# One feed forward moved from an X phase to a Y phase, and the first norm of layer 0 applied after the transpose

## The reference

```python
emb = silu(_sin_emb(timestep)) @ W_ada + b_ada
scale, shift = split(emb)                       # one pair of rows per sequence
x = _ln(src) * (1.0 + scale) + shift            # the first norm; x is also the residual
q, k, v = heads(x @ Wq + bq), heads(x @ Wk + bk), heads(x @ Wv + bv)
scores = q / sqrt(16) @ k.T + attention_bias    # (4, 16, 512, 512), read from HBM
probs = softmax(where(src_mask, -inf, scores))
x = x + (probs @ v) @ Wo + bo
h = _ln(x) * g2 + beta2
x = x + (z * sigmoid(1.702 * z)) @ W2 + b2      # z = h @ W1 + b1, 1024 wide
```

## Time and profile before

| what | before |
|---|---|
| median of 3 runs | 956.56 us |
| lowest, highest | 955.17, 959.86 us |
| the profiled execution, its own time | 951.38 us |
| its span | 949.7 us |
| mean granted clock of PE | 0.935 of full |

### The profile page before, as it was taken

The page is one execution under the profiler, slowest core; times in us unless marked ns, Lnnn a source line. Parts: engine busy times, 40 slices in busy tenths (PEclk is TensorE's granted clock), DMA queues, the critical chain, the costliest instruction groups (busy, mean ns, idle before and its releaser), DMA issues.

```text
span 949.7 us, 14619 instructions
## 1 busy us (share of the span) xinstructions
PE 816.6 (86%) x4856; PEld 488.1 (51%) x4856; DVE 584.7 (62%) x1677; ACT 493.9 (52%) x881; POOL 424.8 (45%) x437
## 2 busy tenths in 40 slices
...
GB/s 237 175 224 250 268 264 178 150 123 146 163 137 2 1 68 156 116 197 224 173 146 45 2 114 173 126 209 202 130 48 46 45 68 150 29 1 2 1 23 22
DMA packets 80046, 114.75 MB, mean 121 GB/s; under 512 B 7691, under 2 KB 43359, under 8 KB 79971
## 3 DMA queue, kind: packets, MB, share of 16 engines
...
## 4 chain that ended last, share of the span: by engine, by line
PE 60%; DVE 17%; issue 7%; ACT 6%; DMA 4%; POOL 3%; SPq 2%; DVEq 0%; ACTq 0%
PE psD L924 11%; PE psD L936 11%; PE psE L958 7%; PE psC L971 5%; PE psS L950 4%; PE psC L1016 4%; PE psD L896 4%; DMA qk<-work 3%; PE psD L912 3%; DVE tiles L1374 3%; POOL tiles L561 2%; PE psS L986 2%; PE psE L1004 2%; PE psD L903 2%; DVE junk L1389 2%
## 5 line engine op out<-in xcount | busy, mean ns | idle before, releaser
L561 POOL TENSOR_TENSOR tiles<-tiles,mask_neg 128x512 f32<-128x512 f32 x256 | 300.3, 1203 | 62.3 <-DMA tiles<-in_fside_Bx16xSxS 47.2
L1374 DVE CUSTOM_DVE_ANT_0 tiles<-psS,tiles 128x512 f32<-128x512 f32 x256 | 173.7, 687 | 131.8 <-PE psS L950 115.0
L696 ACT ACTIVATE prob<-psE 128x512 f32<-128x512 f32 x256 | 151.5, 598 | 88.8 <-PE psE L958 81.6
L687 ACT ACTIVATE tiles<-tiles,rmax 128x512 f32<-128x512 f32 x224 | 162.3, 726 | 48.2 <-DVE rmax L1374 47.5
L958 PE MATMUL psE<-ident,tiles 128*128 128x128 f32 x1024 | 159.1, 278 | 10.9 <-ACT prob L696 10.5
L958 PEld LDWEIGHTS psE<-ident,tiles 128*128 128x128 f32 x1024 | 125.7, 143 | 61.8 <-ACT prob L696 29.5
L936 PE MATMUL psD<-w,work 128*128 128x256 f32 x512 | 132.9, 386 | 3.4 <-ACT hT L739 2.4
L924 PE MATMUL psD<-hT,w 128*128 128x512 f32 x256 | 127.3, 618 | 9.3 <-DVE work L1340 5.9
L602 POOL TENSOR_SCALAR_AFFINE_SELECT prob<-prob 128x256 f32<-128x256 f32 x128 | 50.1, 415 | 185.4 <-ACT prob L708 185.4
L1389 DVE CUSTOM_DVE_ANT_0 junk<-psS,later 128x128 bf16<-128x128 f32 x192 | 82.2, 443 | 76.2 <-PE psS L986 75.5
L950 PE MATMUL psS<-qk 96*128 96x512 bf16 x256 | 100.5, 395 | 22.7 <-DVE rmax L1374 15.4
...
## 6 DMA issues: line engine op xcount, KB each, us to landing
tiles<-in_fside_Bx16xSxS SPq DMA_DIRECT2D x256, 256.0 KB, 3.0
...
qk<-mT SPq DMA_DIRECT2D x64, 3.0 KB
...
```

The costliest lines, as they stand in the source:

```text
L561: pool.tensor_tensor(tile(b, s), tile(b, s), mask_neg[:, tile_of(s)[1], :], ALU.add).then_inc(masked, 1)
L687: act.activation(tile(b, s), tile(b, s), ACT.Identity, scale=-1.0, bias=rmax[0][:, s:s + 1]).then_inc(shifted_a, 1)
L696: act.activation(prob0[:, part_no % 2, j, :, s % 2 * P:(s % 2 + 1) * P], psE[:, e_no(0, b, s) % 2, :].rearrange("p (k q) -> p k q", k=T), ...
L1374: dve.tensor_tensor_reduce(tile(b, s), psS[:, n % 2, :], tile(b, s), 1.0, -3e38, ALU.add, ALU.max, rmax[0][:, s:s + 1]).then_inc(s_drained, 1)
```

## The change

1. **Plan.** The FFN of layer 0, sequence 1, stands in Y0 (slots 20 to 54) and no longer in X1. In Y0 the transposes T1 go from slot 31 to 57, QK from 33, 37, 41, 45 to 58, 61, 64, 67, V from 46, 48 to 72, 76, T2 from 29 to 19. In X1 T1 goes from 49 to 30, QK from 50, 52, 54, 56 to 32, 36, 40, 44, V from 58, 60 to 50, 54. Other phases have slots moved a little. ("ahead of that phase's projections": F1 and F2 are issued before T1 and QK.)
2. **First norm of layer 0.** DVE writes only the normed rows, into `xh` (`normalise`, as in all other norms). PE transposes `xh`; ACT applies scale and shift while it drains, from `ada_col`, a turned copy of scale and shift that four small transposes at the start make for all sequences. The residual `res[b]` is now made on POOL (`modulate`): `xh` times scale, bias of O added to the shift row, and that row added. DVE's next norm waits until POOL and PE have read `xh`.
3. **Start.** `ada_rows(0)` and `keep_ada(0)` stand behind the QK products, the mask of sequence 0 (`turn_mask`) behind `normalise`, and the POOL memsets behind `inv_std`.
4. **SP.** In Y0 and Y1 the first half of the role copies stands ahead of the last `max_rows`. The weights of the next FFN are loaded in Y0.

```diff
 ("start", 0)
-  pre=(0, 0), ln=0, ada=0, t1=2, qk=4, qk_by=2, v=(12, 14)
+  pre=(0, 0), ln=0, ada=11, t1=2, qk=4, qk_by=2, v=(12, 14)
 ("Y", 0)
-  tail=(0, 1), turn=2, out=(9, 10), ln2=13, t2=29, x1=53, masks=41, pre=(0, 2), ln=19, ada=14, t1=31, qk=33, qk_by=4, v=(46, 48)
+  tail=(0, 1), turn=2, out=(9, 10), ln2=13, t2=19, ffn=(0, 1), f1=(20, 22, 24, 26, 28, 30, 32, 34), step=0, f2=(37, 46), per=2, x1=56, masks=44, pre=(0, 2), ln=22, ada=17, t1=57, qk=58, qk_by=3, v=(72, 76)
 ("X", 1)
-  tail=(1, 0), turn=4, out=(9, 13), ln2=17, t2=27, ffn=(0, 1), f1=(1, 3, 5, 7, 10, 13, 15, 17), step=0, f2=(17, 29), per=2, pre=(1, 1), ln=40, t1=49, qk=50, qk_by=2, v=(58, 60)
+  tail=(1, 0), turn=2, out=(9, 13), ln2=17, t2=27, pre=(1, 1), ln=22, t1=30, qk=32, qk_by=4, v=(50, 54)
...
 in_y (SP):
-                if at.ffn and b < B - 1:
+                if at.ffn and at.ffn[0] and b < B - 1:
                     store(at.ffn[1])
+                if at.pre and not at.pre[0]:
+                    to_roles(*at.pre, 0)
                 max_rows(b, 3)
...
                 if at.pre:
-                    for c in range(C):
-                        to_roles(*at.pre, c)
+                    if at.pre[0]:
+                        to_roles(*at.pre, 0)
+                    to_roles(*at.pre, 1)
 POOL:
+            def modulate(b):
+                pool.wait_ge(norm_ready, T * (NORMS.index((0, b, 0)) + 1))
+                wait_emptied(pool, 0, b, "ada", 0)
+                pool.tensor_tensor(res[b][:, :, :], xh[:, :, :], ada[:, 0:D].unsqueeze(1).to_broadcast([P, T, D]), ALU.mult).then_inc(rows_scaled, 1)
+                pool.wait_ge(rows_in, N_ROWS)
+                pool.tensor_tensor(ada[:, D:2 * D], ada[:, D:2 * D], bo_all[0][:, :], ALU.add).then_inc(shift_set, 1)
+                pool.wait_ge(rows_scaled, b + 1)
+                pool.wait_ge(shift_set, b + 1)
+                add_row(res[b], res[b], ada[:, D:2 * D], bo_added)
...
                 inv_std(l, b, 0)
                 if not l:
-                    yield at.t1 + 2
-                    add_bo(b)
+                    yield at.t1 + 2 if at.tail else STEPS - MASK_AHEAD
+                    modulate(b)
 ACT, keep_turned:
-                        scale, shift = 1.0, 0.0
+                        scale, shift = (ada_col[:, x * C + c, b:b + 1] for x in range(2))
 DVE, normalise:
+                if n and half == 0:
+                    pl, pb, second = NORMS[n - 1]
+                    wait_bank(dve, pl, pb, "T2" if second else "T1", C - 1)
+                    if not pl and not second:
+                        dve.wait_ge(rows_scaled, pb + 1)
 DVE, projections:
-                        yield max(at.ln + 4, at.ada + 2) + 2 * half
-                        modulate(b, half)
+                        yield max(at.ln + 4, at.t2 + 2 if at.tail else 0) + 2 * half
+                        normalise(0, b, 0, res[b], half)
```

More of the change, by code:

```diff
@@ L83 @@
 PLANS = {
-    ("start", 0): Plan(pre=(0, 0), ln=0, ada=0, t1=2, qk=4, qk_by=2, v=(12, 14)),
-    ("X", -1): Plan(pre=(0, 1), ln=3, ada=5, t1=14, qk=16, qk_by=4),
-    ("X", 0): Plan(tail=(0, 0), turn=5, out=(9, 10), late=(0, 1, (3, 4)), ln2=13, t2=18, ffn=(0, 0), f1=(21, 22, 24, 25, 27, 28, 31, 31), step=0, f2=(34, 41), per=3.0, pre=(1, 0), ln=50, t1=57, qk=58, qk_by=2, v=(65, 67)),
-    ("Y", 0): Plan(tail=(0, 1), turn=2, out=(9, 10), ln2=13, t2=29, x1=53, masks=41, pre=(0, 2), ln=19, ada=14, t1=31, qk=33, qk_by=4, v=(46, 48)),
@@ new lines @@
+    ("X", -1): Plan(pre=(0, 1), ln=6, ada=5, t1=14, qk=16, qk_by=4),
+    ("X", 0): Plan(tail=(0, 0), turn=5, out=(9, 10), late=(0, 1, (3, 4)), ln2=13, t2=18, ffn=(0, 0), f1=(21, 22, 24, 25, 27, 28, 31, 31), step=0, f2=(34, 43), per=3.0, pre=(1, 0), ln=50, t1=57, qk=58, qk_by=2, v=(65, 67)),
+    ("Y", 0): Plan(tail=(0, 1), turn=2, out=(9, 10), ln2=13, t2=19, ffn=(0, 1), f1=(20, 22, 24, 26, 28, 30, 32, 34), step=0, f2=(37, 46), per=2, x1=56, masks=44, pre=(0, 2), ln=22, ada=17, t1=57, qk=58, qk_by=3, v=(72, 76)),
```

73 lines of the change are left out of this document (33 added, 40 removed).

## The result

| | before | after |
|---|---|---|
| median, same chip, 4 runs each | 955.87 us (952.57 to 959.86) | 944.38 us (940.15 to 946.79) |
| ratio, with its 95% interval | | 0.9877 [0.9852, 0.9902] |
| profiled execution: time, span | 951.38, 949.7 us | 943.82, 942.1 us |
| mean granted clock of it | 0.935 | 0.944 |

The forecast was 938.7 us, 926 to 953: faster, as forecast, and inside the range, but by 11.5 us of the medians (7.6 of the two profiled spans) where 17.9 were forecast. The ratios rest on undisturbed executions alone, and since the one profiled execution of experiment 1's kernel was a slow one (954.23 us), no phase of it is used.

A forecast was written before the change was run, and what follows sets the result against it. TensorE was taken as full in X1, with room in Y0, where DVE was crowded and the clock low. Terms -23.6 + 10.0 - 2.3 - 0.7 - 1.3 = -17.9 gave 933.5 us profiled, 938.7 as median; range 926 to 953.

The forecast's parts named there:

- the two large terms: X1 without the feed forward, -23.6 us, and Y0 with it, +10.0 us.
- the small ones: Start -2.3 us, X-1 -0.7 us, and Y1 with the boundary to X2 -1.3 us.
- 82.6 / 0.886: X1: PE's remaining work of 82.6 us over the busy share 0.886 from X-1 between 72 and 131 us, giving 93.2 us.
- X1 over 100: X1: a sign that the forecast is wrong, if the phase lasts over 100 us; 90 to 97 would show it right.
- I take these to cancel: Y0: twelve split instructions of DVE leave the crowded stretch, the gates' 10.4 us replace them; net effect put at nothing.
- the 3 us on top of Y1: Y0: added to Y1's 97.2 us for gates on DVE, the second norm's earlier transposes and POOL's modulation, giving 100.2 us.
- The slower rival: Y0: the feed forward runs at the low clock, 55.4 us for 27.7; Y0 +40, total 968.7 us; chance 0.05.
- a clock of 0.5 in Y0's FFN: Y0: a sign that the forecast is wrong, TensorE's granted clock at 0.5 during the feed forward.
- Start, -2.3 forecast: Start: eight modulation instructions become four and the mask moves behind, 1.5 + 1.5 us saved; the ada copy costs 0.7.
- X-1, -0.7 forecast: X-1: a POOL bias add of 2.4 us leaves the mask stream; modulation and mask at the end cost 1.7.
- that rival: Y0: PE waits 7 us for max rows behind six role copies on SyncE, total 945.7 us; chance 0.04.
- GpSimd's passes hold DVE: Rival: POOL's longer norm passes stop DVE 3 us at each of four places, 12 us, total 950.7; chance 0.04.

The follow-up runs named there:

- experiment 1: The kernel after with the feed forward back in X1 (Y0 and X1 plan rows of before, T2 of Y0 at 19), new norm kept: 947.29 us, 0.9914 of before.
- experiment 2: The kernel before with only the feed forward moved to Y0 (X1's norm at slot 24), norm and start as before: 956.62 us, 1.0028 of before.
- experiment 3: The kernel after with X1's norm at slot 24 in place of 22: 944.41 us, 0.9896 of before.
- experiment 8: The kernel after with X1's norm at slot 24 and 20 useless matmuls keeping TensorE busy at the X0 to Y0 boundary: 944.90 us, 0.9867 of before.

## Why the prediction was right, and where its terms were off

- **Direction and range: right.** It came out of two errors that partly cancel. Against the forecast sum of -17.9, the two large terms gave +1.7 in place of -13.6, the small ones -9.2 in place of -4.3. That the time fell inside the range is in part luck: with the large terms as measured and the small ones as forecast, the sum is -2.6 and the time 954.0 us, just outside it. The forecast's main mechanism, that the move gives most of the gain, was wrong: by experiment 2 the move alone gives none.
- **X1, -23.6 forecast, -15.0 measured: mis-sized.** The step was "82.6 / 0.886". PE's work, 82.6, is 84.7 where the clock held (experiment 3) and 88.1 where it fell. The share is 0.862 and 0.866, between X-1's whole (0.83) and its good part (0.886) in the earlier trace rows. I had taken the clock of that good part, 1.00, with the share. In X1, with the feed forward gone, PE waits up to 1.93 us at a time for DVE's maxima where two norms meet, and in that stretch the clock falls: 3.6 us of the 8.6 missing, by experiment 3's X1; that the waits make it fall is not shown. The bound of -15.2, X-1's whole length, is what came. The condition "X1 over 100" of the wrong side was met, at 101.8; it holds in executions with the dip, not in those without.
- **Y0, +10.0 forecast, +16.7 measured: mis-sized.** Two steps failed. "I take these to cancel" was said of the projections that move to slots 58 to 76. I had argued there from DVE's idle time alone; the part after slot 56 got 8.7 us longer for 7.6 us more PE work. The forecast took Y1's length, and Y1's part behind about its slot 56 is 28.6 us, Y0's now 33.6. And the 3 us on top of Y1 did not contain the clock at Y0's beginning: it is 0.50 after 4.6 us of standing still at the boundary, 1.6 to 2.9 us by experiment 8, and at half clock again for the first F1 group, 1.9 us. Y0 came out 9.7 us over before's Y1 (97.2), and 5.0, up to 2.9 and 1.9 us are about that; that they add up so is an estimate, not shown.
- **The slower rival** (the feed forward at the low clock) is right in its mechanism for one group out of eight; from 290 us on the clock was 0.96 and over, as I had said would show the forecast right. It had put 40 us on Y0. By this one group the sign "a clock of 0.5 in Y0's FFN" was met as well.
- **Start, -2.3 forecast, -2.4 measured: right in size, one of two steps did not pay.** Four norms in 1.38 us in place of eight instructions in 3.5 us gave 2.1. The mask's 1.5 us off the path gave nothing, since the norm starts at 18.55 us where the modulation started at 18.52. In its place stand one short DVE instruction on the mask's rows (L1233), which lasted 1.32 us instead of 0.18, until GpSimd's memset beside it ended (at 16.63 us; by the change the memsets stand behind `inv_std`), and the copy of the turned ada columns, 0.22 us of wait and 0.18. The transposes end 1.8 us earlier, the last split of q and k 1.4 us, and the other 1.0 us came behind it, between that split and the first scores, where the role copies run; why is open.
- **X-1, -0.7 forecast, -5.6 with X0: wrong in its cause.** I priced GpSimd's passes and left DVE's own length at nothing. From X-1's first turn to its 17th it went from 26.5 to 20.5 us, where DVE's 9.7 us became 3.2. So the term put at nothing without a reason was DVE's time for the norm between the maxima. The modulation at the end came as forecast, 6.7 us from GpSimd's last mask of sequence 0 to its first of sequence 1, and DVE's mask beside it took 3.81 us, against some 1.9 for four elsewhere:

```profile
115.32 8.08 POOL L567 TENSOR_TENSOR tiles<-tiles,mask_neg 128x512 f32<-128x512 f32 x7
123.36 2.38 POOL L581 TENSOR_TENSOR res<-xh,ada 128x1024 f32<-128x1024 f32 x1
...
126.20 3.81 DVE L1242 TENSOR_SCALAR mask_neg<-mask_u,mask_row 128x512 bf16<-128x512 uint8 x4
...
130.09 12.49 POOL L567 TENSOR_TENSOR tiles<-tiles,mask_neg 128x512 f32<-128x512 f32 x11 [1.16 <-DVE mask_neg L1242]
```

- **Y1 and its boundary, -1.3 forecast, -1.1 measured.** PE's wait for the role copies is gone; PE's timeline shows one for ScalarE in its place, nearly as long:

```profile
565.56 0.65 PE L957 MATMUL psS<-qk 96*128 96x512 bf16 x2 [1.06 <-ACT prob L715]
```

  So the phase's own 1.1 us came from inside it, not from this boundary: right in size, not in place. The size hangs on the execution: Y1 was 96.1 to 96.9 us in the nine kernels with the new order and 97.2 to 100.7 in the four without, so it did get shorter, by anything from 0.3 us on. PE did not wait for max rows in Y0, so that rival fell.
- **GpSimd's passes hold DVE: seen, not decided in size.** At the end of X-1 they cost DVE's mask the 1.9 us above. In X1 DVE's L1301 took 1.81 us for two beside GpSimd's masks, where its median is 0.41 for one. The rival had put 12 us on the four places. No kernel with the modulation at another slot was run.
